# A decoder layer on one core: the down-projection over two weight pairs with five shared PSUM banks, and norm means from GpSimd sums

## The reference

```
x = x + attn(layernorm(x))       # RMS norm, Mamba scan, out-projection, RMS norm, gated MLP
x = x + xattn(layernorm(x))      # two int8 smooth-quantized products per sequence
x = x + ffn(layernorm(x))        # gated FFN with 4-bit weights

# inside attn
h   = res + mamba(rmsnorm(res));  hn = rmsnorm(h)
mlp = (silu(hn @ gate_w.T) * (hn @ up_w.T)) @ down_w.T      # 2048 hidden
# inside ffn
gate = x @ dequant(Wg).T;  up = x @ dequant(Wu).T           # 4096 hidden
out  = (gelu(gate) * up) @ dequant(Wd).T
```

## Time and profile before

| | us |
|---|---|
| median of 3 runs | 3127.9 (3126.78 to 3128.18) |
| profiled execution | 3122.57 |
| its span, first to last instruction | 3120.8 |
| busy: TensorE / VectorE / ScalarE / GpSimd | 2763.6 / 2285.1 / 1158.0 / 1099.5 |

### The profile page before, as it was taken

The page is one execution under the profiler, slowest core; times in us unless marked ns, Lnnn a source line. Parts: engine busy times, 40 slices in busy tenths (PEclk is TensorE's granted clock), DMA queues, the critical chain, the costliest instruction groups (busy, mean ns, idle before and its releaser), DMA issues.

```text
span 3120.8 us, 32784 instructions
## 1 busy us (share of the span) xinstructions
PE 2763.6 (89%) x11248; PEld 1932.1 (62%) x11248; DVE 2285.1 (73%) x2903; ACT 1158.0 (37%) x1668; POOL 1099.5 (35%) x776
## 2 busy tenths in 40 slices
PE   6488898888888857999999999899999999999998
PEld 2344444444444235778777777777777777777777
DVE  6599999999999954444476667777776666676664
ACT  3355555555555433332244433332332321222221
POOL 0288888888888811010000001111111111212210
PEclk8798998888889668999999999999999999999999
DMA  3554555456455254011111012112111111111111
GB/s 131 179 171 143 161 150 155 142 158 163 130 171 145 58 212 155 21 68 61 61 41 59 23 41 61 41 41 61 39 39 37 29 56 46 42 41 41 42 55 59
DMA packets 152215, 275.37 MB, mean 88 GB/s; under 512 B 27248, under 2 KB 27760, under 8 KB 151536
## 3 DMA queue, kind: packets, MB, share of 16 engines
q1 hardware_dynamic: 152048, 273.27, 28.6%
HBM read 178.27 MB, written 61.34 MB: 77 GB/s over the span
## 4 chain that ended last, share of the span: by engine, by line
PE 47%; DVE 21%; ACT 10%; SPq 7%; issue 6%; POOL 6%; DMA 3%; DVEq 0%; POOLq 0%; ACTq 0%
PE ps L1508 11%; PE ps L1510 10%; PE ps L1509 10%; PE ps L1548 7%; ACT ps L764 4%; PE ps L1558 4%; DVE state L1165 4%; SPq L603 3%; POOL wdeq L1053 3%; DVE alo L1460 2%; PE ps L1620 2%; POOL read L1019 2%; DVE prod L1454 2%; DVE glo L1228 2%; SPq L607 1%
## 5 line engine op out<-in xcount | busy, mean ns | idle before, releaser
L1053 POOL TENSOR_TENSOR wdeq<-packed,scales 128x1024 f32<-128x1024 f16 x96 | 229.7, 2392 | 1454.4 <-DVE packed L1285 1020.9
L1019 POOL TENSOR_TENSOR read<-state,c_t 128x512 f32<-128x512 f32 x512 | 655.1, 1291 | 141.2 <-DVE state L1165 117.5
L1165 DVE TENSOR_TENSOR_SCAN state<-ps,drive 128x512 f32<-128x512 f32 x512 | 618.3, 1208 | 14.1 <-ACT ps L764 13.1
L1508 PE MATMUL ps<-xh,ghi 128*128 128x512 f32 x1536 | 609.1, 397 | 1.7 <-DVE res L1220 0.9
L1510 PE MATMUL ps<-xh,glo 128*128 128x512 f32 x1536 | 598.4, 390 | 0.0
L1509 PE MATMUL ps<-xl,ghi 128*128 128x512 f32 x1536 | 598.1, 389 | 0.0
L764 ACT ACTIVATE ps<-ps,a_exp 128x512 f32<-128x512 f32 x512 | 338.9, 662 | 468.2 <-PE ps L1548 467.2
L1508 PE MATMUL ps<-ahi,ghi 128*128 128x512 f32 x768 | 323.1, 421 | 93.3 <-DVE res L1439 74.8
L1439 DVE TENSOR_TENSOR res<-res,ps 128x512 f32<-128x512 f32 x384 | 258.7, 684 | 184.5 <-PE ps L1510 183.9
L1156 DVE TENSOR_TENSOR drive<-ps,b_t 128x512 f32<-128x512 f32 x512 | 339.8, 664 | 21.7 <-PE ps L1548 21.1
L1548 PE MATMUL ps<-dpack,sel 128*128 128x512 f32 x512 | 261.0, 510 | 103.9 <-DVE state L1165 102.3
(11 more groups left out here) (167 smaller groups left out, 3709.5 us busy)
## 6 DMA issues: line engine op xcount, KB each, us to landing
whi<-w_d SPq DMA_DIRECT2D x63, 256.0 KB, 3.9
wlo<-w_d SPq DMA_DIRECT2D x63, 256.0 KB, 4.8
x_d<-ev SPq DMA_DIRECT2D x32, 256.0 KB, 3.1
x_t<-x_d SPq DMA_DIRECT2D x32, 256.0 KB, 4.8
b_d<-ev SPq DMA_DIRECT2D x32, 256.0 KB
b_t<-b_d SPq DMA_DIRECT2D x32, 256.0 KB, 4.0
c_d<-ev SPq DMA_DIRECT2D x32, 256.0 KB, 3.0
c_t<-c_d SPq DMA_DIRECT2D x32, 256.0 KB, 3.2
```

Source lines behind the costliest of these rows:

```text
L1019: pool.tensor_tensor(read[:, n % RRING, :], state[:, n % SRING, :], c_t[:, g % 2, :], ALU.mult).then_inc(read_ready, 1)
L1053: pool.tensor_tensor(wdeq[:, :].rearrange("p (h n) -> p h n", h=2), codes, scale, ALU.mult).then_inc(deq, 1)
L1165: dve.tensor_tensor_scan(state[:, n % SRING, :], ps[:, n % 2, :], drive[:, n % DRING, :], 0.0, ALU.mult, ALU.add)\
L1508: pe.matmul(out_, w_h, x_h, start=(start and k == 0), stop=False)
```

## The change

The down-projection is done once for two pairs. A double pair E has 24 positions: 16 for gate and up of eight activations, then 8 for down, one bank each, with four unit tiles x three passes = 12 matmuls. So a down bank is added half as often. All positions take the banks 0 to 4 in turn (`free_bank(V) = V % 5`), and a position waits for the reader of the position five earlier (`bank_taken`). `prod` is gone, the product is written over `act_o`, so `act_o` of U waits for `alo` of U - 2. There are four `ahi`/`alo` buffers.

The weights are handled by the tile T (six per double pair: gate, up, gate, up, down, down), in a ring of five high and low tiles (`WRING`) with two load buffers. Tile T is loaded at p = 4T - 19, unpacked at 4T - 14, dequantized at 4T - 13, split at 4T - 12 and 4T - 11. A quantized tile's load is 9 DMAs. In the out-projection the third tile is made at m = 10 and 11 rather than 6 and 7.

The mean is one matmul: GpSimd first adds the channel tiles in pairs and then the two sums (`sum_tiles`), and TensorE multiplies the result with `mean_w`. The sums are new background steps of GpSimd (`attend_sum`, `norm_sum`, `rms_sum`); the other engines' steps shift by one or two (`x_step`, `n_step`), `X_LEN` grows to 37, and `rms_var` and what follows it moves one chunk or position later. GpSimd's adding of the input x (`add_input`) for sequences 2 and 3 gets a place in its list of positions.

```diff
+WRING = 5
+X_LEN = 37
+        def tile_of(T):
+            E, k = divmod(T, 6)
+            return (2 * E + k // 2, k % 2) if k < 4 else (2 * E + k - 4, 2)
+        def prepared_at(p, off):
+            T, rest = divmod(p + 12 - off, 4)
+            return [T] if rest == 0 and 3 <= T < ALL_T else []
+        def free_bank(V):
+            return V % 5
...
+            def load_tile(T):
+                if T >= MLP_T + 2:
+                    sp.wait_ge(deq, T - MLP_T - 1)
+                elif T >= 2:
+                    sp.wait_ge(w_lo, T - 1)
...
-                    if m == OCH * b + 8:
+                    if m == OCH * b + 9:
                         rms_step(b, 2)
...
                     if U >= 2:
-                        act.wait_ge(prod_done, U - 1)
-                    act.activation(act_o[U % 2][:, :], ps[:, (2 * U) % 3, :],
+                        act.wait_ge(a_lo, U - 1)
+                    act.activation(act_o[U % 2][:, :], ps[:, free_bank(24 * E + i - 1), :],
...
+            def sum_tiles(dst, src, signal):
+                pair_done[0] += 1
+                pool.tensor_tensor(dst[:, 0:2, :], src[:, 0:2, :], src[:, 2:4, :], ALU.add)\
+                    .then_inc(pairs_summed, 1)
+                pool.wait_ge(pairs_summed, pair_done[0])
+                pool.tensor_tensor(dst[:, 0, :], dst[:, 0, :], dst[:, 1, :], ALU.add).then_inc(signal, 1)
+            def attend_sum(b, r):
+                if r == 0:
+                    pool.wait_ge(added, 8 * MLP_E * (h + 1) - 4 + 4 * (b % 2))
...
+                if i >= 17:
+                    add_down(E, i - 17)
+                for T in prepared_at(p, -2):
+                    if T >= MLP_T:
+                        unpack(T)
+                for T in prepared_at(p, 1):
+                    w_low(T)
...
-            def mean(g, src):
-                for f in range(FT):
-                    last = pe.matmul(ps[:, bank_of(g), :], mean_w[:, :], src(f), start=(f == 0),
-                                     stop=(f == FT - 1))
-                last.then_inc(bg_ready, 1)
+            def mean(g, summed):
+                pe.matmul(ps[:, bank_of(g), :], mean_w[:, :], summed[:, 0, :], start=True, stop=True)\
+                    .then_inc(bg_ready, 1)
...
+            def bank_taken(V):
+                if V >= 5:
+                    E, i = divmod(V - 5, 24)
+                    if i >= 16:
+                        pe.wait_ge(added, 8 * E + i - 15)
+                    elif i % 2:
+                        pe.wait_ge(prod_done, 8 * E + i // 2 + 1)
+                    else:
+                        pe.wait_ge(act_done, 8 * E + i // 2 + 1)
+                return ps[:, free_bank(V), :]
...
+                    if i == 16:
+                        pe.wait_ge(w_lo, 6 * E + 6)
+                    if f == 0:
+                        pe.wait_ge(a_lo, 8 * E + 7 + bb)
+                    d = [((6 * E + 4 + j // 2) % WRING, D * (j % 2) + P * f) for j in range(4)]
+                    three_pass(bank_taken(p), [
+                        (ghi[s][:, at:at + P], glo[s][:, at:at + P],
+                         ahi[j][:, cols(bb)], alo[j][:, cols(bb)]) for j, (s, at) in enumerate(d)])\
+                        .then_inc(down_ready, 1)
```

More of the change, by code:

```diff
@@ L384, in stage, with load_count @@
             return True, (Q - MLP_Q) // FFN_PAIRS, (Q - MLP_Q) % FFN_PAIRS
+        def tile_of(T):
[6 more added lines that the diff above has]
+            return V % 5
+        def load_count(T):
+            return sum(16 if u < MLP_T else 144 for u in range(T % 2, T + 1, 2))
         def background(p):
@@ L1037, in _, with add_input @@
             phase_end(pool, 2)
-            for b in range(B):
+            def add_input(b):
                 pool.wait_ge(r_scaled, b + 1)
@@ new lines, in norm_sum @@
+            def norm_sum(b, r):
+                if r == 0:
+                    pool.wait_ge(attended, 2 * (b // 2) + 2)
+                    sum_tiles(xlr[b], res[:, :, cols(b)], e["n_summed"])
+                if r == 4:
+                    pool.wait_ge(e["n_squared"], b + 1)
+                    sum_tiles(xhr[b], xhr[b], e["n_summed"])
+            rms_sum(0)
+            rms_sum(1)
+            add_input(0)
+            add_input(1)
+            for p in range(24 * ALL_E):
+                for b in (2, 3):
+                    if p == 12 * (b - 2) + 1:
+                        rms_sum(b)
+                    if p == 12 * (b - 2) + 28:
+                        add_input(b)
+                for T in prepared_at(p, -1):
+                    if T >= MLP_T:
+                        dequantize(T)
+                for h, r in background(p):
+                    for bb in range(2):
+                        attend_sum(2 * h + bb, r - X_LEN * bb)
+                    for bb in range(2):
+                        norm_sum(2 * h + bb, r - 2 * X_LEN - 2 - bb)
@@ L1442, in _ @@
-            for p in range(12 * ALL_Q + 1):
-                Q, i = divmod(p, 12)
-                if i == 0 and Q:
-                    add_down(8 * Q - 2)
-                    add_down(8 * Q - 1)
-                if Q == ALL_Q:
+                dve.tensor_tensor(res[:, f, cols(b)], res[:, f, cols(b)],
+                                  ps[:, free_bank(24 * E + 16 + k), :], ALU.add).then_inc(added, 1)
+            for p in range(24 * ALL_E + 1):
+                E, i = divmod(p, 24)
+                if i == 0 and E:
+                    add_down(E - 1, 7)
+                if E == ALL_E:
```

351 lines of the change are left out of this document (174 added, 177 removed).

## The result

The changed kernel takes 2954.9 us (2952.4 to 2957.5, 4 runs) against 3127.3: the ratio is 0.945, with a 95% interval from 0.943 to 0.947, a gain of 172 us. The forecast was 2974 and the range 2945 to 3022.

What follows compares the result with a forecast made beforehand. TensorE was taken to bound the loop: 1567 us of matmuls, 15 of means, 70 of other background and 45 of waits gave 1697. With 8 us off the out-projection and 5.3 for the median: 2970, put at 2974 (2945 to 3022).

Steps and rivals of the forecast that it cites:

- The signs: Loop: idle ahead of down matmuls under 30 us, none for adds; 40 mean records; clock 0.99; matmuls 0.2267 us apart.
- The bound: Loop: TensorE bounds it; 6912 three-pass matmuls at 0.2267 us, 1567 us, stay as they are.
- The means: Norm means in the loop: one f32 matmul for four, 18 x 2.57 = 46 us less, 15 us left.
- (b): Loop: background transposes and int8 products, without the means, take 70 us of TensorE.
- (c): Loop: TensorE's waiting and its wake at the lower clock, 148 us before the change, 45 us after.
- The adds' waits: Down-projection: the 74.8 us of waits for adds into `res` go, with most of the 37 us clock loss.
- Tile-wise weights: Weight handling in the loop: work unchanged, VectorE's wait for scales off the path, costed at nothing.
- Out-projection: Stage before the loop: 8 us gained, between 0 and 12, from shorter means and adds done beforehand.
- Alo: FFN double pairs: down phase waits for alo, 1.1 us 16 times plus clock, 35 us, 3009 us; chance 0.14.
- Chain: Loop: GpSimd's sums delay TensorE at 16 uses, 2.5 us each with the clock, about 3005 us; chance 0.12.
- Bank waits stay: Down-projection: five banks only move the wait; means and out-projection alone count, 3074 us; chance 0.06.
- Slower by the tile buffers' round: FFN weight tiles: the two load buffers' round stretches beyond 21.8 us; at 26 us, 3176 us; chance 0.04.

Runs made afterwards that it cites:

- e1: The changed kernel with its means as four f32 matmuls again and no GpSimd sums; 2997.6 us.
- e2: The kernel before, with gate, up and down taking five banks in turn instead of three and two; 3071.8 us.
- e7: The kernel before with five banks, and the FFN's scales loaded for its first pair alone; 3009.9 us.
- e8: The kernel before with its two down banks, and the FFN's scales loaded for its first pair alone; 3093.2 us.
- e11: The changed kernel with a VectorE copy of a PSUM bank ahead of the seventh alo in the last eight double pairs; 2964.8 us.
- e4: The changed kernel with a third GpSimd operation, an add of 1024 columns, in each of the 20 sums; 2971.4 us.

## Why the prediction was right

**The signs.** All came: 20.2 us ahead of the down matmuls (under 30), none for an add, 40 mean records, a clock of 0.99 in the loop, 0.2267 us a matmul, and no gate or up matmul in the loop waits for a bank.

**The bound.** 0.2267 us a matmul and 1567 us of it stand: the nine double pairs from 2362 us on take 65.28 us each but for the end, which is 288 x 0.2267 and nothing else.

**The means.** Forecast 46 us in the loop; 46.0 in matmul time, 42.0 with the sums' effect (e1). I had put the sums' cost at 11 us, 6 for the chain and 5 for the path; it measured about 4, of which 0.3 us is a wait ahead of a mean. The 15 us that the sum leaves for the means are right too, but they stand in two places: 8.5 us from their own starts to the next, and 7.3 in the matmul behind each mean. A mean's second record starts 0.03 us before that matmul, whose own interval is then 0.63 us instead of 0.23.

**Other background, (b).** I took 70 us from busy times, in which the background's short matmuls overlap. From start to start they hold 59 us after the change, with 6 us of waits inside, and 68 before, with 11. Another 7 us stand in the intervals of the matmuls right behind them, as with the means; whether these belong to the background as well, no run shows. So (b) was 4 to 11 us too large.

**What stays of (c).** The loop's 1683.5 us less 1567 for the three-pass matmuls, 8.5 for the means and 59 for the background leave 49: 20.2 us of waits ahead of down, 2 of waits ahead of means and background, and 27 of longer intervals. Of the 27, 14 are those right behind means and background, and about 6 are lost in the loop's four stretches at 1.2 GHz, 20.5 us in all. Before the change there were 20 of them, 78.5 us, and 33 us lost: the clock loss that I had put at 37 us went with the waits, as forecast. Without the means' 7.3 us, (c) is 42 us against 45 forecast. These 3 us and the 11 between 59 and 70 in (b) are what the loop was forecast too long (1697 against 1683.5 us). The make-up was different. The 10 us of start costs, 0.4 per double pair, do not exist in pairs without background; in return the down phase's start in pairs with background cost more.

**The adds' waits.** They all went, as forecast, and "what is late next is the start of the down phase" was right. It was not priced for the ring alone: e2 shows that there 57.5 of the 93.3 us of idle time ahead of down stay.

**Tile-wise weights: the step that failed.** I costed them at nothing and called VectorE's wait for scales off the path. e7 and e8 show it on the path: 62 us with five banks and 35 with two. The sum came out because I let all waits for adds go, whatever their cause. That was luck in so far as the change cured both causes at once. A forecast for the ring alone would have been wrong by this, as e2's was. What the tile-wise loads are worth in the changed kernel itself is not measured: no run has it with pair-wise loads.

**Out-projection.** 8 us forecast, 5.5 measured, and nearly all of it the two shorter means (2 x 2.57 = 5.1). The stand did not shrink: the two waits of 8.17 us for adds are gone, but waits for VectorE's `ulo` grew in their place, and TensorE's waits between the stage's first matmul and the loop's are 24.2 us before and 24.8 after.

**The rivals.** Alo: the wait priced right and the clock too high, the condition not met in the pairs without background (e11). Chain: not met, but at four of 18 uses the sums are at its edge (e4). Bank waits stay: no, the adds' waits are gone; but its mechanism, that five banks only move the wait, is what e2 shows for more than half of it on the old kernel. Slower by the tile buffers' round: no sign; before the change, not after it, the loads' round was what came late.

**The median.** I carried the 5.3 us between profiled execution and median over; after the change the median lies 2.6 us below. These 8 us, the 13 of the loop and the 4 that I added to the sum, less 5 or 6 for the out-projection and the stage before, make the 19 us between 2974 and 2954.9.

## What to carry to other kernels

When an engine waits for a buffer, ask why its reader is late before adding buffers: here about half of the bank waits in the pairs without background came from a chain of loads three engines away, and five banks alone moved the wait to the next deadline. In an in-order list, what stands between a product and the step that the bounding engine waits for matters more than the list's total; moving the weights' preparation by two places was worth 17 us with the same work. Take an engine's time from start to start where its instructions overlap, not from busy sums, and look at the interval behind a stretch too: part of the stretch's time can stand there.

## What the hardware showed

Which of VectorE and GpSimd waited on their shared path went by what VectorE had running when the dequantization came: an alo listed 0.17 us ahead of it took 0.68 us and lengthened it to 2.78, one behind a PSUM read took 2.50 us and left it at 2.39. A memset that started 0.03 us before a dequantization was followed by an alo that did not wait either, with the dequantization at 3.26 us; why is left open. That VectorE passes the path on to whatever it runs next is not the general case: the clip at 2180.18 us (1.22 us) held the dequantization up, and wqbf, listed 0.04 us behind the clip's end, then waited for it and took 3.25 us. A blocked operation's listed time ends after the other's by nearly its own length: 0.55 us for alo (0.69 alone), 1.08 for wqbf (1.23 alone).
